# Adding the squares of two channel halves on VectorE before the mean product of an output norm

## The reference, cut to what matters

```python
def _ln(x, w, b, eps=1e-05):
    mu = x.mean(-1, keepdims=True)
    var = x.var(-1, keepdims=True)
    return (x - mu) / jnp.sqrt(var + eps) * w + b
...
y = y.reshape(b, DI, h, w_).transpose(0, 2, 3, 1)
y = _ln(y, out_norm_w, out_norm_b) * _silu(z)
attn = jnp.einsum('bhwd,cd->bhwc', y, out_proj_w)
x = shortcut * skip_scale + attn
xl = _ln(x, ln2_w, ln2_b).transpose(0, 3, 1, 2)
```

## Time and profile before

| | us |
|---|---|
| median of 3 runs | 12892.73 |
| the runs | 12888.64 to 12894.24 |
| the profiled execution, its own time | 12887.85 |
| its span on the core | 12886.1 |
| the norm stage, one image (8 of them) | 66.6 to 69.3 |

### The profile page before, as it was taken

The page is one execution under the profiler, slowest core; times in us unless marked ns, Lnnn a source line. Parts: engine busy times, 40 slices in busy tenths (PEclk is TensorE's granted clock), DMA queues, the critical chain, the costliest instruction groups (busy, mean ns, idle before and its releaser), DMA issues. The chain is left out here.

```text
span 12886.1 us, 117201 instructions
## 1 busy us (share of the span) xinstructions
PE 8781.3 (68%) x25368; PEld 2456.9 (19%) x25368; DVE 11234.5 (87%) x7246; ACT 7092.4 (55%) x9476; POOL 9777.7 (76%) x4212
## 2 busy tenths in 40 slices
PE   7766666666666666666666666666666666588888
PEld 2221111111111111111111111111111111122323
DVE  6759999999999999999999999999999999554544
ACT  6655555555555555555555555555555555355555
POOL 0009999999999999999999999999999999312110
PEclk9877777777777777777777777777777777788888
DMA  4557777777777777777777777777777777434241
GB/s 134 168 169 173 175 176 176 175 176 175 176 174 173 175 177 175 176 176 176 176 175 176 174 172 173 176 176 175 178 176 177 176 176 175 112 75 101 71 100 30
DMA packets 581791, 2060.60 MB, mean 160 GB/s; under 512 B 82647, under 2 KB 87543, under 8 KB 566775
## 3 DMA queue, kind: packets, MB, share of 16 engines
q1 hardware_dynamic: 581366, 2056.93, 69.7%
HBM read 1599.46 MB, written 457.18 MB: 160 GB/s over the span
## 5 line engine op out<-in xcount | busy, mean ns | idle before, releaser
L822 POOL TENSOR_TENSOR dBu<-rep,BC 128x1024 f32<-128x1024 f32 x3072 | 7155.9, 2357 | 988.5 <-DMA rep<-dd_dram 952.1
L618 PE MATMUL py<-hC,fold 128*32 128x512 f32 x12288 | 2959.7, 861 | 2593.7 <-POOL hC L829 2439.1
L667 ACT ACTIVATE pd<-rep,a_now 128x1024 f32<-128x1024 f32 x3072 | 3420.8, 1114 | 1253.4 <-DVE hC L790 1004.0
L782 DVE TENSOR_TENSOR_SCAN pd<-pd,carry,dBu 128x1024 f32<-128x1024 f32 x1536 | 3596.2, 2341 | 0.0
L829 POOL TENSOR_TENSOR hC<-h,BC 128x1024 f32<-128x1024 f32 x1024 | 2402.3, 2346 | 539.1 <-DVE h L782 492.4
L790 DVE TENSOR_TENSOR hC<-pd,BC 128x1024 f32<-128x1024 f32 x2048 | 2507.6, 1224 | 169.6 <-DVE pd L782 29.2
L782 DVE TENSOR_TENSOR_SCAN h<-pd,carry,dBu 128x1024 f32<-128x1024 f32 x768 | 1798.4, 2342 | 0.0
L679 ACT ACTIVATE carry<-pd 128x1 f32<-128x1 f32 x1536 | 262.0, 171 | 2701.8 <-DVE hC L790 2571.6
L618 PEld LDWEIGHTS py<-hC,fold 128*32 128x32 f32 x12288 | 516.5, 138 | 4811.3 <-POOL hC L829 3210.6
L782 DVE TENSOR_TENSOR_SCAN pd<-pd,dBu 128x1024 f32<-128x1024 f32 x512 | 1168.1, 2282 | 38.4 <-issue 19.3
L587 PE MATMUL pp<-xdbl,w_dt 38*96 38x512 f32 x1024 | 712.3, 830 | 490.2 <-ACT xdbl L687 487.7
(11 more groups left out here) (153 smaller groups left out, 8974.3 us busy)
## 6 DMA issues: line engine op xcount, KB each, us to landing
rep<-dd_dram SPq DMA_DIRECT2D x1024, 768.0 KB, 12.8
BC<-bc_dram SPq DMA_DIRECT2D x2048, 256.0 KB, 9.0
u_dram<-p_u SPq DMA_DIRECT2D x64, 1536.0 KB, 17.6
u<-u_dram SPq DMA_DIRECT2D x128, 768.0 KB, 5.3
dd_dram<-LG SPq DMA_DIRECT2D x256, 384.0 KB, 4.5
dd_dram<-RL SPq DMA_DIRECT2D x256, 384.0 KB, 3.0
y_dram<-y SPq DMA_DIRECT2D x256, 384.0 KB, 11.1
p_y<-y_dram SPq DMA_DIRECT2D x61, 1536.0 KB, 16.0
```

Source lines behind the costliest of these rows:

```text
L618: last = mm(py[32 * g:32 * g + 32, t2(t)], fold[:, :], hC[:, j % 2 * 3 + g, t2(t)], start=(j % 4 == 0), stop=(j % 4 == 3), skip_group_chec ...
L667: go(pd[:, i % 2, :], rep[:, half, 0, g, :], ACT.Exp, scale=a_now[:, i:i + 1]).then_inc(S.exped, 1)
L782: v.tensor_tensor_scan(dst, pd[:, i % 2, :], dBu[:, i % 4, :], carry[:, i:i + 1] if c else 0.0, ALU.mult, ALU.add).then_inc(S.scanned, 1)
L822: nc.gpsimd.tensor_tensor(dBu[:, i % 4, :], rep[:, half, 1, g, :], BC[:, s, 0, r, :], ALU.mult).then_inc(S.dbu, 1)
```

## The change

VectorE gets one more instruction for each tile: `pair_squares(b, t)` waits for the square of tile t and adds the second half of `SQ` onto the first, in place. `var_y(t)` waits for this sum (`y_paired`) in place of `y_squared`, and makes one product from it. `pair_squares(b, 0)` stands behind `center_y(b, 0)`; `pair_squares(b, i + 1)` stands at the end of VectorE's step i, behind the gate of tile i.

```diff
                 def var_y(t):
                     n = b * NT + t
-                    pe.wait_ge(S.y_squared, done(n + 1))
+                    pe.wait_ge(S.y_paired, done(n + 1))
                     pe.wait_ge(S.y_log, done(n))
-                    for half in range(2):
-                        last = mm(ps[0:HALF, 4, :], mean2[:, :], SQ[:, t % 2, half * PT:(half + 1) * PT],
-                                  start=(half == 0), stop=(half == 1))
-                    last.then_inc(S.y_var, 1)
+                    mm(ps[0:HALF, 4, :], mean2[:, :], SQ[:, t % 2, 0:PT], start=True, stop=True).then_inc(S.y_var, 1)
...
+            def pair_squares(b, t):
+                n = b * NT + t
+                dve.wait_ge(S.y_squared, done(n + 1))
+                v.tensor_tensor(SQ[:, t % 2, 0:PT], SQ[:, t % 2, 0:PT], SQ[:, t % 2, PT:2 * PT],
+                                ALU.add).then_inc(S.y_paired, 1)
+
             def body(b, more):
                 center_y(b, 0)
+                pair_squares(b, 0)
                 for i in range(NT + 3):
...
                         last.then_inc(S.gated, 1)
+                    if i + 1 < NT:
+                        pair_squares(b, i + 1)
```

More of the change, by code:

```diff
@@ L57 @@
 bc_loaded0 bc_loaded1 bc_loaded2 bc_loaded3 dd_stored rep_loaded0 rep_loaded1 a_picked skipped
-added hc_dve hc_pool out_stored0 out_stored1 x3_loaded0 x3_loaded1 y_meaned
+added hc_dve hc_pool out_stored0 out_stored1 x3_loaded0 x3_loaded1 y_meaned y_paired
 conv_pe x_loaded4 x_loaded5 x_loaded6 x_loaded7
```

## The result

| | before | changed |
|---|---|---|
| median, us (10 runs each) | 12892.08 | 12917.73 |
| the runs, us | 12885.79 to 12900.51 | 12910.93 to 12938.89 |
| profiled execution, its span, us | 12886.1 | 12916.2 |

A forecast was written before the change was run, and what follows sets the result against it. The prediction saw two limits in the steady round, TensorE's products (6.88 us) and a dependency loop (6.87 us). Its sum: 8 x (2.4 head - 0.4 tail + 1.3 clock) = 26.4, say +27 on 12892.7: 12920 us, range 12903 to 12940.

The forecast's parts named there:

- Steady rounds, 0 gained: Middle of the stage: the round stays at 6.8 to 6.9 us although each tile loses a 0.86 us product.
- both limits: Middle of the stage: TensorE's eight products, 6.88 us, and a dependency loop from project to project without var_y, 6.87 us.
- The sum, 0.69 us and hidden in VectorE's wait: Steady part: the added VectorE sum takes 0.69 us inside its 0.93 us wait for project, some 0.3 us left.
- Rival 3: Head of the stage: slower by more, the sum taking 1.24 us (12933) or the clock staying half longer (12931); chance 0.18.
- Head, +2.4 us by the place of the sum: Head of the stage: sums queued behind VectorE's gates delay var_y(1), var_y(2) and so project(1), costing 2.4 us per image.
- Clock in the head, +1.3: Head of the stage: two new TensorE waits lower its clock, 1.3 us per image, the middle between 0 and 2.7.
- the upper bound: Head of the stage: all five products between the two waits run at 1.2 GHz, costing 2.7 us per image.
- Tail, -0.4: Last tiles of the stage: 0.5 us gained per image, less 0.1 for longer products in five rounds.
- The two short gains: Tail: one product less brings Ln and Exp forward, gaining 0.22 us, then about 0.3 one tile later.
- The stages behind unchanged: After the changed stage: the following stages keep their length.
- Rival 1: Head of the stage: it costs time but the clock holds, 8 x 2.0 = 16 us, 12909 us; chance 0.22.
- Rival 2: Steady rounds: TensorE is the bound, each full round gains 0.86 us, 34 us in all, 12858 us; chance 0.05.

The follow-up runs named there:

- e1: Kernel before, with var_y making one product on the first half of the squares and no sum on VectorE; 12890.42 us, ratio 1.0002.
- e5: Kernel before, with two PSUM banks in turn for center_x and y's deviation moved into SBUF; 12864.92 us, ratio 0.9984.
- e6: Changed kernel, with two PSUM banks in turn for center_x and y's deviation moved into SBUF; 12865.48 us, ratio 0.9987.
- e8: Changed kernel, with four products nobody reads added in TensorE's waits ahead of var_y(1) and var_y(2); 12922.35 us, ratio 1.0032.
- e3: Changed kernel, with the change for tiles 0 to 2 only; tiles 3 to 7 keep two products and no sum; 12916.28 us, ratio 1.0028.
- e10: Kernel before, with five products nobody reads added in TensorE's waits in the tail of the stage; 12854.88 us, ratio 0.9966.
- e4: Changed kernel, with the second product of var_y put back beside the sum; 12936.91 us, ratio 1.0041.

## Why the prediction came out

The forecast was 12920 us, the measurement 12917.73, and the ratio lies where the forecast had it, close to the 0.2% that the prediction took as what can be told from no change (the interval, 1.0013 to 1.0032, does not include 1). By its steps:

- **Steady rounds, 0 gained.** Right, and the step on which most hung: 20.67 us from `project(1)` to `project(4)` before and after, and e1, e5, e6 show both limits apart. A row of TensorE without gaps had hidden a second limit 0.01 us away.
- **The sum, 0.69 us and hidden in VectorE's wait.** Right: 0.68 us, 0.30 us of wait left. Rival 3's 1.24 us did not occur.
- **Head, +2.4 us by the place of the sum.** Right: `var_y(1)` +2.51 against +2.52 forecast, both in image 2; `project(1)` +2.3 with the clock held (e8); e3 carries it all.
- **Clock in the head, +1.3.** Right in kind and nearly in size: 1.2 (changed kernel against e8). The middle between two bounds was a guess that happened to fall near. In image 2 not all five products behind the first wait ran slow, as the upper bound had it, but `var_y(1)` and about half of `mean_y(3)`, for 1.91 + 2.81 us where 1.10 + 1.88 is the full pace.
- **Tail, -0.4.** Wrong: +0.58 to the last `var_x`. The two short gains are there (in image 3 from `project(4)` to `project(5)` 6.17 us against 6.39, from `center_x(5)` to `project(6)` 2.69 against 2.95, together 0.49). What the step left out is the clock: it took TensorE's clock in the tail to stay as it was. In the tail of the kernel before the clock already falls behind TensorE's waits, and with the waits filled it does not (e10); a shorter product leaves TensorE idle for longer there; e1, with the product gone and nothing else, lengthens the tail by 1.94 us. That is not the whole cause, since e3 lengthens it by 1.11 us and e4 by 0.45 with both products in place. In the changed kernel the clock falls in image 2 during `var_x(4)` and `project(5)`, two tiles earlier than before (the earlier trace rows had it at `var_x(6)`); so it does in one more of the eight images, while in image 3 it falls at `var_x(6)` and is still down at the last `var_x`. TensorE's timeline in image 2:

```profile
11405.39 1.39 PE L1009 MATMUL p_ps<-p_sq,p_mean 96*96 96x512 f32 x2 [0.68 <-ACT p_sq L1193]
11406.58 3.33 PE L994 MATMUL p_ps<-p_yn,p_w_out 96*96 96x512 f32 x4
```

- **TensorE's busy time smaller by 64 products of 0.86 us**, which is 55 us. Wrong: on the page it fell from 8781.3 us before to 8763.7, by 17.6. The products that are left ran at the half clock more often (granted clock 0.92 before and 0.87 now, as the mean of the eight stretches from the first product to the end of the last `var_x`) and count for longer; this is the likely reason, not shown apart.
- **The stages behind unchanged.** Not quite: 0.5 us per image came back by L1369. The two misses, +1.0 in the tail and -0.5 behind it, partly cancel; 8 x 3.52 = 28 us in the profiled execution, 26 on the medians. That the total met the forecast to 2 us is luck within this.

Rival 1 (clock holds) falls, since the clock took its part in the head. Rival 2 falls by e1. The prediction took the rule of the Trainium skill, page "Perfetto Trace Analysis", section "Identifying the Most-Contended Engine" (optimize the engine with the highest occupancy first), by TensorE's busy time. The same section excepts TensorE from this: its headroom is to be judged by MFU and by the busy share of its weight loads. The prediction left that out, and by weight loads TensorE stood at 20.91 of 69.30 us, under VectorE's 42.98. So by its weight loads TensorE was not the engine to start with (its MFU was not worked out). Read by TensorE's busy time the rule would have had the round shorter, and the trace disagrees with that reading: 6.89 us before and after, and only with the dependency loop eased as well does the round fall to 6.23.

What stays open: what sets the moment at which the clock falls in the tail. In e8 it falls earlier than in the changed kernel, whose code its tail has, and in e3 it stays down for longer than before, with the tail's code of before; the tails of both begin at another time, behind a head that ran otherwise, and no run parts the two.

## What to carry to other kernels

A full engine is one limit; before taking work from it, sum the loop of waits that passes by the removed instruction, and if it is as long as the round, ease both or neither (and ask whether both are worth it: here e6 was no faster than e5). A new instruction in an in-order list costs at the head of a pipeline, where nothing is queued to hide it, even if the steady state has room: here three tiles of eight made all of the loss. Work removed from TensorE in a stretch with waits can lower its clock and slow what remains (e1), and so can a change ahead of that stretch (e3); look at the granted clock of the neighbouring stretches before counting the gain.

## What the runs showed of the hardware beyond expectation

Idle products in waits paid for themselves: the kernel before with five more products per image is 0.34% faster (e10). The granted clock of the stage went to 0.96, from 0.89 in image 2, and the products of the tail ran at 2.4 GHz. Half of the gain came behind the stage. Of the 4.7 us by which L1369 comes earlier, 2.5 are there at the end of the last `var_x`, and 2.2 are won in the convolutions (47.1 us against 49.3 from there to L1369, mean over the images), which e10 did not touch. Image 2, columns as in the earlier trace rows, before and then in e10:

```profile
11418.60:11467.90 49.30, 42.08 (x211) 13.58 (x210) 11.00 (x11) 27.55 (x48) 15.48 (x7) 0.88 0.56 128
11415.90:11462.80 46.90, 39.75 (x210) 13.55 (x210) 12.28 (x10) 27.47 (x47) 12.83 (x6) 0.93 0.49 107
```

The granted clock there is 0.93 in place of 0.88.

The same wait need not bring the same clock. In the changed kernel the wait ahead of `var_y(1)` is 3.25 us in images 2 and 5. In image 2 the product behind it took 1.91 us; in image 5 it took 1.10, and the clock fell only during `mean_y(3)` (3.31 us for two products in place of 1.88):

```profile
12036.30 1.10 PE L987 MATMUL p_ps<-p_sq,p_mean 96*96 96x512 f32 x2 [3.25 <-DVE p_sq L1323]
12037.23 3.31 PE L980 MATMUL p_ps<-p_acc,p_mean 96*96 96x512 f32 x4
```
